# First attention of a four-layer transformer kernel: the value products of a step move from units 3 and 7 into one group in unit 5

## The reference

```
q = einsum('bnd,hde->bhne', query, Wq) / sqrt(64)
k = einsum('bmd,hde->bhme', query, Wk)
v = einsum('bmd,hde->bhme', query, Wv)
attn = softmax(einsum('bhne,bhme->bhnm', q, k), axis=-1)
out  = einsum('bhnm,bhme->bnhe', attn, v)
out  = swapaxes(out, -1, -2).reshape(B, N, E * H) @ Wp + bp
```

## Time and profile before

| | |
|---|---|
| runs of the kernel | 1186.91, 1187.3, 1188.91 us; median 1187.3 us |
| the profiled execution | 1186.8 us, with a span of 1184.8 us between its first and last instruction |
| first attention's steps | from about 48 us to about 735 us of the span |
| busy in the whole span | TensorE 89%, VectorE 75%, ScalarE 62%, GpSimd 57% |

### The profile page before, as it was taken

The page is one execution under the profiler, slowest core; times in us unless marked ns, Lnnn a source line. Parts: engine busy times, 40 slices in busy tenths (PEclk is TensorE's granted clock), DMA queues, the critical chain, the costliest instruction groups (busy, mean ns, idle before and its releaser), DMA issues. The chain is left out here.

```text
span 1184.8 us, 25711 instructions
## 1 busy us (share of the span) xinstructions
PE 1053.6 (89%) x7981; PEld 849.6 (72%) x7981; DVE 894.0 (75%) x1768; ACT 734.1 (62%) x1367; POOL 671.6 (57%) x667
## 2 busy tenths in 40 slices
PE   6889999999999999999999998568974898999996
PEld 5678888888888888888888886345853666666664
DVE  5877887787787788788778774666756488899997
ACT  4556666666666666666666665544443777777774
POOL 4266676676676676667667666110320676676772
PEclk9999999999999999999999999798997899999998
DMA  5333534444353353443434330100001202221101
GB/s 117 68 75 75 117 72 100 98 89 96 78 114 81 67 122 73 89 109 77 102 83 103 83 76 4 47 1 1 1 1 39 80 13 65 80 69 53 53 1 36
DMA packets 57720, 80.18 MB, mean 68 GB/s; under 512 B 26515, under 2 KB 38734, under 8 KB 56654
## 3 DMA queue, kind: packets, MB, share of 16 engines
q1 hardware_dynamic: 55478, 79.17, 28.3%
q10 hardware_dynamic: 2208, 0.59, 0.3%
HBM read 19.63 MB, written 1.11 MB: 18 GB/s over the span
## 5 line engine op out<-in xcount | busy, mean ns | idle before, releaser
L596 POOL TENSOR_TENSOR probs_lo<-probs 128x512 f16<-128x512 f32 x384 | 393.8, 1043 | 248.5 <-ACT probs L439 247.3
L460 DVE TENSOR_REDUCE maxes<-bank_m 128x1 f32<-128x512 f32 x512 | 348.9, 689 | 82.6 <-PE bank_m L268 76.1
L439 ACT ACTIVATE probs<-bank_s 128x512 f32<-128x512 f32 x512 | 305.1, 600 | 86.8 <-PE bank_s L356 61.8
L1228 POOL TENSOR_TENSOR hidden_lo<-hidden,hidden_hi 128x512 fp32r<-128x512 f32 x111 | 173.5, 1585 | 92.5 <-ACT hidden_hi L1377 92.2
L349 PE MATMUL bank_s<-qa,ka 128*128 128x512 f32 x512 | 217.8, 425 | 3.0 <-DVE v_parts L507 2.5
L268 PE MATMUL bank_m<-ka,qa 128*128 128x512 f32 x512 | 211.1, 412 | 6.2 <-DMA ka<-tk_lo 3.9
L356 PE MATMUL bank_s<-qb,kb 65*128 65x512 f32 x512 | 205.6, 402 | 1.2 <-DMA qb<-negmax 1.2
L291 PE MATMUL bank_o<-v_now,probs 128*128 128x129 f16 x2048 | 200.6, 220 | 1.4 <-DVE probs_lo L536 1.3
L291 PEld LDWEIGHTS bank_o<-v_now,probs 128*128 128x128 bf16 x2048 | 175.4, 97 | 22.3 <-issue 20.7
L268 PEld LDWEIGHTS bank_m<-ka,qa 128*128 128x128 f32 x512 | 158.6, 310 | 38.5 <-DVE maxes L460 12.6
L287 PE MATMUL bank_o<-v_now,probs_lo 128*128 128x65 f16 x2048 | 184.6, 193 | 0.0
(11 more groups left out here) (226 smaller groups left out, 1591.9 us busy)
## 6 DMA issues: line engine op xcount, KB each, us to landing
qa<-tq_hi SPq DMA_DIRECT2D x64, 256.0 KB, 4.0
v_now<-v_parts SPq DMA_DIRECT2D x32, 260.0 KB, 2.3
ka<-tk_hi SPq DMA_DIRECT2D x32, 256.0 KB, 2.9
ka<-tk_lo SPq DMA_DIRECT2D x32, 256.0 KB, 4.9
kb<-tk_hi SPq DMA_DIRECT2D x32, 256.0 KB, 5.0
qb<-tq_lo SPq DMA_DIRECT2D x32, 256.0 KB, 5.1
gates_on_all<-gate_rows SPq DMA_DIRECT2D x8, 1024.0 KB, 4.7
e_raw<-in_L_ffn_ew_dram SPq DMA_DIRECT2D x16, 256.0 KB, 5.2
```

The source lines that it names most:

```text
L439: nc.scalar.activation(probs[:, c, u, :], bank_s[u % 2][:], ACT.Exp, scale=SCALE).then_inc(exp_done, 1)
L460: nc.vector.tensor_reduce(maxes[:, j // 2, j % 2:j % 2 + 1], bank_m[j % 2][:], AX.X, ALU.max).then_inc(m_reduced, 1)
L596: nc.gpsimd.tensor_tensor(probs_lo[:, c, u, :], p, hi, ALU.subtract).then_inc(lo_pool, 1)
L1228: nc.gpsimd.tensor_tensor(h_lo[:, f, :], h[:, f, :], h_hi[:, f, :].bitcast(F32), ALU.subtract).then_inc(lo_pool, 1)
```

## The change

All 32 sets of value products run in unit 5. Both groups of inversions move to unit 5, all four `take_o` to the beginning of unit 6, and the two places that handled the group of unit 7 go away. The same instructions are issued on each engine, in another order. The only wait that goes or comes is bound to those places: `o_added` is now waited for ahead of all four `take_o`.

```diff
-    PV_TO = [0, 0, 0, 16, 16, 16, 16, 32]
-    GROUPS_AT = {3: (0, 1), 7: (2, 3)}
+    PV_TO = [0, 0, 0, 0, 0, 32, 32, 32]
+    GROUPS_AT = {5: (0, 1, 2, 3)}
@@ scalar: step
-                    if u == 0 and not (first and s < 2):
-                        bi, bs = (i, s - 2) if s >= 2 else (i - 1, s + 2)
-                        for qt in GROUPS_AT[UNITS - 1]:
-                            take_o(bi, bs, qt)
                     if u and u - 1 in GROUPS_AT and not (first and s == 0):
@@ scalar: after
-                for qt in GROUPS_AT[UNITS - 1]:
-                    take_o(i - 1, 2, qt)
                 act.wait_ge(o_added, 4 * i - 2)
```

## The result

The changed kernel takes 1321.81 us (median of 4 runs, 1319.55 to 1323.5), the kernel before 1188.11 us (median of 4 runs, 1186.91 to 1189.11): a ratio of 1.1125, 95% interval 1.11 to 1.1149. It is 11% slower. The forecast was 1308 us, in a range of 1257 to 1326.

The account below looks back on a forecast made before the run. TensorE sets the pace, so every added wait counts in full. Waits of 11.25 us and work of 39.5 less 0.3 make a pair 50.45, 7.95 more; 15 turns (119) plus 2 outside give 1308 us, range 1257 to 1326.

Parts of the forecast that it names:

- wait up to the group of step 0: Unit 5 of step 0: TensorE stands 2.8 us for the head load, with 4.87 left of the 7.39 it needs.
- second projection: In step 1, TensorE waits 1.7 us for VectorE's make_lo in place of 1.1, as the value products in between are gone.
- wait up to the group of step 2: Unit 5 of step 2: TensorE waits 3.15 us for the head load, with 4.47 between last scores and use.
- tile 2, step 2: Query tile 2 of the group in step 2: TensorE stands 0.2 us for the bank of the value products.
- L268 in step 3: Unit 2 of step 3: L268 waits 0.55 us, because unit 7's uncovered probs_lo comes ahead of unit 0's reduce.
- tile 2, step 3: Query tile 2 of step 3: 0.9 us, as unit 3's probs_lo makes the first inversion late.
- VectorE's work without cover: Steps 1 and 3: uncovered probs_lo delays reduces and first inversions, 0.8 us at tile 2 of step 1, 1.45 in step 3.
- The bank: Value products, four query tiles together: with VectorE and ScalarE free, TensorE stands 0.2 us at query tile 2.
- The clock: Rival: TensorE's 30 stands each cost 1.5 us of half clock work, 45 more, 1353 us; 4 in 100, including unlisted waits.
- The bank alone: Rival: head loads in time and VectorE keeps up; only 0.2 us at each of 62 steps, 1199 us; 5 in 100.
- faster: Rival: four fewer restarts a pair and small waits in steps 2 and 3 vanish, 1169 us; 2 in 100.
- The head load hidden: Rival: both head waits go but VectorE's delays under them return, 3.4 us a pair, 1257 us; 10 in 100.

Follow-up runs that it names:

- run 1: The changed kernel with head transfers behind the first pair cut to 128 of 1024 columns: 1264.67 us, ratio 1.0657.
- run 2: The kernel before with head transfers behind the first pair cut to 128 of 1024 columns: 1187.03 us, ratio 0.9997.
- run 4: The changed kernel with the whole group of 32 sets in unit 3 instead of unit 5: 1253.3 us, ratio 1.0556.
- run 7: The kernel before with all 32 sets in one group in unit 7: 1241.62 us, ratio 1.0441.
- run 5: The changed kernel with VectorE's two probs_lo of a step (units 3 and 7) given to GpSimd: 1295.94 us, ratio 1.0907.
- run 12: The changed kernel, full head transfers, with all probs_lo on GpSimd except that of unit 5, on VectorE: 1295.11 us, ratio 1.0902.
- run 6: The changed kernel with six extra matmuls of 512 columns ahead of the head wait of step 2: 1309.46 us, ratio 1.1012.
- run 9: The changed kernel with head transfers cut to 128 of 1024 columns behind the first pair and all probs_lo on GpSimd: 1245.48 us, ratio 1.048.
- run 11: The changed kernel with head transfers cut to 128 columns behind the first pair, probs_lo on GpSimd except unit 5's, on VectorE: 1239.26 us, ratio 1.043.

## Why the prediction was right, point by point

The mechanism held, and so did the sum but for the clock: at full clock a pair takes 50.5 us, against 50.45 in the forecast. The time lay 14 us above the forecast, inside the range. Its terms against the pair from 353.46 us on in the trace of the changed kernel, read as in the prediction (distance on TensorE less its own work):

| term | predicted us | measured us |
|---|---|---|
| wait up to the group of step 0 | 2.8 | 353.46 to 362.30, 8.84 - 6.16 = 2.7 |
| tile 2, step 0 | 0.2 | 2.91 - 2.74 = 0.2 |
| second projection | 1.7 | 370.63 - 369.00 = 1.6 |
| third projection | 0.95 | 373.68 - 372.74 = 0.9 |
| tile 2, step 1 | 0.8 | 380.36 - 376.94 - 2.74 = 0.7 |
| wait up to the group of step 2 | 3.15 | 380.36 to 390.98, 10.62 - 7.31 = 3.3 |
| tile 2, step 2 | 0.2 | 395.24 - 390.98 - 2.74 = 1.5, at half clock; in the next pair 445.83 - 442.92 - 2.74 = 0.2 |
| L268 in step 3 | 0.55 | 0.5 |
| tile 2, step 3 | 0.9 | 405.48 - 401.50 - 2.74 = 1.2 |
| sum | 11.25 | 12.6 |

The only large difference, at tile 2 of step 2, is the clock; tile 2 of step 3 came out 0.3 high, and every other term within 0.15.

- **The head load is the largest part.** Shown by runs 1 and 2: 57 us of the 134 go when the transfers are short (12 of them the clock behind the stands), and the same edit does nothing to the kernel before. That place decides is shown by runs 4 and 7, where the same group costs 66 and 53 us instead of 134. In step 0 the load began 0.43 us after the last scores of step 3 (354.51 to 354.94), not 0.65, and landed 7.15 behind them instead of 7.39; TensorE went on 0.4 after the landing, where I had put 0.3. Together that is the 0.1 by which 2.7 lies below 2.8.
- **VectorE's work without cover.** Shown by runs 5 and 12: 2.6 us a pair at full clock, of an expected 2.7. In the change, `probs_lo` of unit 3 in step 3 lasted 1.41 us beside GpSimd, not 0.98, and so tile 2 of that step cost 1.2 instead of 0.9. In the distances for the reduce, the 0.95 is 0.93 (332.98 - 332.05); nothing hangs on it.
- **The bank.** 0.2 us where nothing else is late, as the earlier trace rows had it.
- **The clock** was the term mis-sized. I had it as a rival with 45 us if every stand cost 1.5. It fell in about every second pair and cost 1.4 there: 11 to 12 us, by run 6. That is most of the 14 us between forecast and result; the rest lies in the steps outside the loop and behind them, put at 2 us and measured at 6 (136.5 less 15 times 8.7). The page "TensorE: Matmul & The Clock Gate" of the Trainium skill (Part 1) has the clock halve after idleness. The trace agrees, but does not say when: TensorE stood 1.9 us ahead of the matmul at 390.42, where the clock fell, and as long ahead of the same matmul one pair later, at 442.46, where it stayed at 1.00. I should have put a part of this price into the forecast itself.
- **A step that was incomplete.** I wrote that `o_pair` and the transposes were not waited for and that what comes earlier saves nothing. In the change TensorE does stand at the transposes of step 0 (the first row of its waits above). It costs nothing there only because the head load is waited for two units later. Runs 9 and 11 show it by itself: 1.7 to 2.2 us a pair once the other causes are gone.
- **Two signs that came otherwise.** The clock did not stay at full. And L268 of unit 5 has 0.88 and 1.72 us of idle time ahead of it, not near 3 each: part of each wait is spent earlier, at the transposes in step 0 (0.64) and at the reduce in step 2 (0.67).
- **The rivals.** The bank alone (1199) and faster (1169) are out by the result. The head load hidden (1257) is what run 1 built: 1264.67.
- **What stays open.** With heads short and `probs_lo` moved, a pair is 45.4 us and not 42.05. The wait for `o_pair` is about 1.9 of the 3.3; the rest was seen as several waits of 0.2 to 0.5 at tile 2 and L268 of steps 2 and 3, and not taken apart by a run.

## What to carry to other kernels

An order that looks movable may be holding up deadlines of other engines' work: measure from the last use of a buffer to the first use of its refill, and count which work between the two would leave. Here 2.74 of 7.78 us left and the slack was 0.39. A wait that is found can lie on top of others; removing it gives back less than its length, and a stand also costs what TensorE's clock does after it.

## What the runs showed of the hardware

- A stand of TensorE of about 2 us, in a stage where it is otherwise busy, was followed by a granted clock of 0.50 in some pairs and not in others with the same instructions; six matmuls in the stand of step 2 kept it at 1.00 from 108 to 850 us (12 us, run 6).
- VectorE's `probs_lo` (128x512) lasted 0.69 us alone, and 0.98 (before) and 1.41 us (changed kernel) where it began while GpSimd's same operation was running. Where VectorE's began first (388.17 against 388.23 us in the changed kernel), it kept its 0.68 us and GpSimd's lasted 1.51 us instead of 1.04.
- Taking work from VectorE made the changed kernel's pairs shorter and its clock lower (0.960 to 0.946, run 5). Why is not shown. The stands are not the same ones: in a pair of run 5 TensorE's idle time ahead of the transposes is 1.68 us instead of 0.64, and the idle time ahead of unit 5's L268 in step 2 is 2.27 us instead of 1.72.
